# A decoder kernel on one core: the grouped attention stage with another order on TensorE, and moved preparation, rounding and end

## The chip, the cores and the metric

The kernel runs as one program on one core of a Trainium2 chip. The metric is device time in microseconds (us) of one execution. The median of three runs before the change is 1420.6 us (1420.59 to 1421.44). The engines are TensorE (PE in the profile, with its weight loads as PEld), VectorE (DVE), ScalarE (ACT), GpSimd (POOL) and SyncE (SP, which issues DMAs). They run their own instruction streams and meet only through semaphores.

## The reference, cut to what matters

Two decoder layers on 16 sequences of 128 tokens and 256 features, float32. Six steps follow each other, each adding to the residual x:

```python
x = x + L0_attn(layernorm(x))            # RWKV: token shift, three projections, a running maximum and two scans
x = x + L0_xattn(layernorm(x), ctx, ctx) # grouped attention: 32 query heads, 8 key heads, 8 features a head
x = x + L0_ffn(layernorm(x))             # dense part and 8 experts, top 2
x = x + L1_attn(layernorm(x))            # windowed attention with RoPE, 16 heads of 128
x = x + L1_xattn(layernorm(x), ctx)      # attention on a latent context
x = x + L1_ffn(layernorm(x))
```

The second step, which most of the change is about, is

```python
scores = einsum('bkgsd,bktd->bkgst', qh, kh) / sqrt(8)
out = einsum('bkgst,bktd->bkgsd', softmax(scores), vh)
```

## The kernel before, in words

Each step of the reference is one stage (a function and a block of five instruction streams): `rwkv`, `gqa`, `experts`, `windowed`, `cross` and the last feed forward. A stage begins on all engines when the one before has ended. The order of the work on each engine is written out by hand; a `wait_ge` on a semaphore count stands wherever an engine needs another's result.

**The stage `gqa`** runs over 16 blocks t of 128 tokens; each block has two halves of 16 heads, so 32 halves n. For each half: DVE normalises the block (`normalise`, L941, once a block), POOL splits it into a rounded and a rest part (`split_h`, L772 and L773), PE turns it (`turn_head`, L834), ACT takes it out of PSUM (`take_head`, L906), PE forms the scores in four pieces j of 512 columns in two PSUM banks in turn (`scores`, L843), DVE takes the extreme of each piece (`minimum`, L950). When both halves of a block are done, DVE splits the extremes in a rounded part (L958, a copy) and a rest (L960) (`split_least`), PE turns them (`turn_least`, L850) and ACT takes them out (`take_least`, L911). Then, three halves later than the scores (LEAD = 3), PE forms the scores again in turned form, less the extremes (`shifted_scores`, L859 and L863), ACT takes the exponents (`weigh`, L916, four per half), PE forms the weighed sums with a column of ones (`attend`, L871, into the one bank O), ACT takes them out (`take_out`, L922), PE turns them back into the same bank O (`turn_out`, L878), and DVE divides by the row sums (`divide`, a reciprocal L969 and a product L972). POOL adds the result to x.

PE's loop in step n is, in order: turned scores of n; scores pieces 0 and 1 of n+3; on odd n the turning of the extremes; weighed sums of n-1; scores piece 2; turning of a head part; scores piece 3; turning of the sums of n-1. `attend(n)` waits for the count `out_read` to reach n, that is for `divide(n-1)`, since bank O is shared. DVE's loop in step n begins with `divide(n-2)`, then the four minima of half n+3 (a normalisation behind the second on even n, a `bn_stats` behind the third on odd n), then on even n `split_least`. POOL's loop over t is: add of block t-2, split of block t+3, a copy of values, the key split of block t+4 and, in blocks 13 and 14, four products that fold norm weights into weights of the next stage (`fold_ffn0`).

The stage opens with the means and variances of all 16 blocks (L192), their scale on POOL, and the first normalisations.

**The stage `windowed`** runs over 16 blocks t with four key heads g. Here the change touches step g = 2 and 3: DVE's `rotate` (a sum L2366, a product with the cosines L2381, two with the sines L2383) and `take_weights` (a copy out of PSUM, L2404), which PE's `attend` (L2186) needs; POOL's `join` (L2062, for keys also L2065), `normalise` (L2072); ACT's `take_attended` (L2294) and `take_turned` (L2278), the latter needed by the scores of the next block (L2174, L2177).

Of the kernel before, what the change touches and what calls it, by code (L numbers as in the profile page):

```python
# [25 lines left out]
P = 128  # L26
# [188 lines left out]
def rwkv(nc, net, sem):  # L215
# [8 lines left out]
    with ExitStack() as ctx:  # L224
# [39 lines left out]
        own_dve, own_pool, own_act = sem("rw_own_dve"), sem("rw_own_pool"), sem("rw_own_act")  # L264
        block = ctx.enter_context(nc.Block("rwkv"))

        @block.sync
        def _(sp):
            load(nc, net)
            sp.wait_ge(net.keys_split, 1)  # L270
            sp.wait_ge(net.zeroed, 1)
            set_keys(sp, net, 0)
            sp.dma_start(net.later_keys[:].bitcast(F32), net.dram["ctx_keys"][:, 4:NB, :]).then_inc(net.keys_in[2], 16)
# [30 lines left out]
        def _(pool):  # L304
# [14 lines left out]
            split_keys(pool, Own(pool, net.own_keys), net, 0)  # L319
# [174 lines left out]
        def _(dve):  # L494
# [56 lines left out]
            def add(g):  # L551
                for i in range(2):
# [6 lines left out]
                    for j in (2 * i, 2 * i + 1):  # L559
                        dve.wait_ge(added, GB * g + j + 1)  # L560
                        dve.bn_stats(net.stats[:, GB * g + j, :], net.x[:, GB * g + j, :])
# [52 lines left out]
            def one(g, first, last):  # L614
# [11 lines left out]
                if not first and not last:  # L626
                    add(g - 1)
                own.again()
# [49 lines left out]
def gqa(nc, net, sem):  # L678
# [10 lines left out]
    VW, HALVES, LEAD = 32, 2 * NB, 3  # L689
    SLOTS, KEYS = 6, 4  # L690
# [4 lines left out]
    with ExitStack() as ctx:  # L695
# [23 lines left out]
        ones_set = sem("gq_ones_set")  # L719
# [18 lines left out]

        def set_by(t):

            return 64 * (t // 2) + 64

        @block.sync
        def _(sp):
            for t in range(1, NB):
                sp.wait_ge(keys_split, t + 1)
                if t >= 2:
                    sp.wait_ge(keys_set[t % 2], set_by(t - 2))
# [7 lines left out]
        def _(pool):  # L756
# [3 lines left out]
            def next_keys(t):  # L760

                if t >= KEYS:
                    pool.wait_ge(keys_set[t % 2], set_by(t - KEYS))
# [23 lines left out]
            scale_of(pool, own, net, scratch, aggregated, rstd_ready, 0, 1, WIDEN)  # L787
            split_h(0)
            scale_of(pool, own, net, scratch, aggregated, rstd_ready, 1, NB, WIDEN)
            pool.memset(least_parts[:].bitcast(F32), 0.0).then_inc(ones_set, 1)  # L790
            pool.wait_ge(net.keys_in[1], 16)
            next_keys(1)
            split_h(1)
            next_keys(2)
            split_h(2)
            pool.memset(values[:], 0.0).then_inc(ones_set, 1)
            pool.wait_ge(ones_set, 2)
            pool.memset(values[:, :, :, HD:HD + 1], 1.0).then_inc(ones_set, 1)
            pool.wait_ge(ones_set, 3)
            pool.wait_ge(net.in_ctx, 16)  # L800
            fetch_values(0)
            next_keys(3)
            for t in range(NB):
# [10 lines left out]
                if t in (NB - 3, NB - 2):  # L814
                    fold_ffn0(pool, net, t - NB + 3)
# [7 lines left out]
        def _(pe):  # L823
# [42 lines left out]
            def attend(n):  # L866
                pe.wait_ge(weighed, 4 * n + 4)
                pe.wait_ge(values_in, n // 2 + 1)
                need(pe, out_read, n)
                for v in range(4):  # L870
                    mm = pe.matmul(ps[32 * v:32 * v + VW, O, :], values[:, n // 2 % 2, 4 * (n % 2) + v, :],  # L871
# [3 lines left out]
            def turn_out(n):  # L875
                pe.wait_ge(out_taken, n + 1)
                for j in range(4):
                    mm = pe.transpose(ps[:, O, j * P:j * P + P], out_t[:, n % 2, j * P:j * P + P], ident)  # L878
                mm.then_inc(out_turned, 1)

            for n in range(-LEAD - 1, HALVES + 1):
                ahead = 0 <= n + LEAD < HALVES
                if 0 <= n < HALVES:
                    shifted_scores(n)
                if ahead:
# [4 lines left out]
                if n >= 1:  # L890
                    attend(n - 1)
# [6 lines left out]
                if n >= 1:  # L898
                    turn_out(n - 1)

        @block.scalar
        def _(act):
# [16 lines left out]
            def take_out(n):  # L919
                act.wait_ge(attended, n + 1)  # L920
                need(act, out_turned, n - 1)
                act.activation(out_t[:, n % 2], ps[:, O, :], ACT.Copy).then_inc(out_taken, 1)  # L922
# [15 lines left out]
        def _(dve):  # L938
# [14 lines left out]
            def split_least(t):  # L953
                parts = least_parts[:, t % 2].rearrange("p j (v c e) -> p c j v e", v=4, e=2)[:, 0:2]
                dve.wait_ge(topped, 8 * t + 8)
                dve.wait_ge(ones_set, 1)
                need(dve, least_turned, t - 1)
                dve.tensor_copy(parts[:, :, :, :, 0], least[:, t % 2]).then_inc(least_high, 1)  # L958
# [4 lines left out]
            def heads():  # L963
                return ps[:, O, :].rearrange("p (j g v) -> p g j v", j=4, v=VW)

            def divide(n):

                dve.wait_ge(out_turned, n + 1)
                dve.reciprocal(rsum[:, n % 2], heads()[:, :, :, HD]).then_inc(inverted, 1)  # L969
                dve.wait_ge(inverted, n + 1)  # L970
                need(dve, added, n // 2)
                dve.tensor_tensor(out[:, n % 2], heads()[:, :, :, 0:HD], wide(rsum[:, n % 2], [P, 4, 4, HD]),  # L972
                                  ALU.mult).then_inc(out_read, 1)

            def measure(t):
# [6 lines left out]
            dve.tensor_reduce(chosen[:], net.const[:, CONST["ident"]].rearrange("p (v c e) -> p c v e", v=4, e=2)[:, 0:2],  # L982
                              AX.XY, ALU.add).then_inc(tables_set, 1)
            dve.wait_ge(tables_set, 1)
            dve.tensor_scalar(minus[:], wide(chosen[:], [P, 2, P]), -1.0, None, ALU.mult).then_inc(tables_set, 1)
            dve.wait_ge(rstd_ready, 2)
            for t in (1, 2):
                normalise(t)
            for n in range(-LEAD, HALVES + 1):
                if n >= 2:  # L990
                    divide(n - 2)
                for j in range(4):
                    if n + LEAD < HALVES:
                        minimum(n + LEAD, j)
                    if j == 1 and n >= 0 and n % 2 == 0 and n // 2 + 3 < NB:
                        normalise(n // 2 + 3)
# [16 lines left out]
def fold_ffn0(pool, net, c):  # L1013

    if c == 0:
        pool.wait_ge(net.in_ffn0, 16 * 6)
    for tile, base, extra in ((net.gate0, PRE1, 1.0), (net.up0, PRE1, 1.0), (net.egu, PRE2, 1.0),
                              (net.router_w, RSCALE, float(D) ** -0.5)):
# [2162 lines left out]
```

## Time and profile before

| | |
|---|---|
| median of three runs | 1420.6 us |
| profiled execution | 1428.85 us |
| its span, first to last instruction | 1427.0 us |
| busy share of the span: PE, DVE, ACT, POOL | 86%, 68%, 53%, 42% |
| mean granted TensorE clock | 0.94 |
| stage `gqa` in the span | 136.8 to 309 us |
| stage `windowed`, its loop | about 600 to 1053 us |

Times of rows are microseconds from the span's start. In a row of the timeline the columns are start, length, engine, line, operation, result and operands, shape and count; in brackets stands how long the engine was idle before it and what ended that. A granted clock of 1.00 is 2.4 GHz, 0.50 is 1.2 GHz.

### The profile page before, as it was taken

What the parts mean: (1) busy time and instruction counts of PE and PEld (TensorE: products, weight loads), DVE (VectorE), ACT (ScalarE), POOL (GpSimd) and SP (SyncE); (2) the same over time, 40 slices, a digit from 0 to 9 for tenths busy, and PEclk for the clock granted to TensorE, in tenths of its full rate; (3) what the DMA queues carried; (4) which work ended last, traced back from release to release, by engine and by line L of the source; (5) the groups of instructions that cost most, each with busy time, mean ns of one, the idle gap of its engine ahead of it and who ended that gap; (6) DMA issues with size and microseconds to landing.
All of it is one profiled execution on the core that took longest, in us unless ns stands there. A gap on an engine that the chain in (4) does not pass through costs nothing. (4 is left out here: it accounts for less than half of the span.)

```text
span 1427.0 us, 24807 instructions
## 1 busy us (share of the span) xinstructions
PE 1228.8 (86%) x7726; PEld 944.8 (66%) x7726; DVE 965.2 (68%) x1864; ACT 760.5 (53%) x1755; POOL 605.0 (42%) x738
## 2 busy tenths in 40 slices
PE   6895899979988976389998999899987899969998
PEld 5673444448878865267776777777764565548887
DVE  5998799845755347877777777777764666643443
ACT  5432577753545455456666666666643555533332
POOL 2001555463055444576667666666653333320000
PEclk9997899968999997599999999999997999979999
DMA  9001000010025314200000000000000000000000
GB/s 326 1 0 48 19 16 16 9 60 1 5 85 156 100 51 167 107 0 1 2 0 0 0 0 0 0 0 0 1 1 4 5 3 3 3 1 1 15 15 31
DMA packets 27422, 44.74 MB, mean 31 GB/s; under 512 B 5648, under 2 KB 22160, under 8 KB 25936
## 3 DMA queue, kind: packets, MB, share of 16 engines
q1 hardware_dynamic: 23888, 34.31, 7.0%
q0 software_dynamic: 3456, 9.44, 2.5%
q8 instruction: 42, 0.69, 0.2%
q14 instruction: 36, 0.29, 0.1%
HBM read 32.21 MB, written 9.44 MB: 29 GB/s over the span
## 5 line engine op out<-in xcount | busy, mean ns | idle before, releaser
L2287 ACT ACTIVATE wi_weights<-wi_psum,wi_bias,wi_scale 128x128 f32<-128x128 f32 x256 | 113.9, 454 | 119.3 <-DVE wi_bias L2397 119.3
L2062 POOL TENSOR_TENSOR wi_straight<-wi_straight,wi_crossed 128x512 f32<-128x512 f32 x80 | 103.5, 1294 | 10.9 <-DVE wi_crossed L2383 10.8
L950 DVE TENSOR_REDUCE gq_least<-gq_psum 128x4 f32<-128x512 f32 x128 | 84.6, 686 | 15.9 <-PE gq_psum L843 14.2
L2050 POOL TENSOR_TENSOR wi_scratch<-wi_sums,wi_eps 128x4 f32<-128x4 f32 x80 | 35.3, 441 | 130.6 <-DVE wi_sums L2366 129.2
L2051 POOL TENSOR_TENSOR wi_scale<-wi_scratch,minus_half 128x4 f32<-128x4 f32 x80 | 84.6, 1058 | 6.3
L2388 DVE TENSOR_REDUCE wi_top<-wi_psum 128x4 f32<-128x512 f32 x64 | 44.0, 687 | 62.5 <-PE wi_psum L2177 62.5
L2186 PE MATMUL wi_psum<-wi_weights_t,wi_values 128*128 128x512 f32 x128 | 67.9, 612 | 20.5 <-DVE wi_weights_t L2404 20.5
L916 ACT ACTIVATE gq_weights_t<-gq_psum 128x512 f32<-128x512 f32 x128 | 67.6, 600 | 28.0 <-PE gq_psum L863 28.0
L2813 DVE TENSOR_REDUCE cr_top<-cr_psum 128x4 f32<-128x512 f32 x64 | 43.7, 682 | 46.2 <-PE cr_psum L2628 46.2
L2072 POOL TENSOR_TENSOR wi_weights<-wi_weights,wi_inverse 128x512 f32<-128x512 f32 x64 | 66.4, 1038 | 9.5 <-remote 5.1
L2177 PEld LDWEIGHTS wi_psum<-wi_k_t,wi_q_t 128*128 128x128 f32 x512 | 68.4, 194 | 1.7
L2177 PE MATMUL wi_psum<-wi_k_t,wi_q_t 128*128 128x128 f32 x512 | 68.0, 276 | 0.0
L2568 POOL TENSOR_TENSOR cr_keys_diagonal<-cr_qk,const 128x256 f32<-128x256 f32 x32 | 19.4, 627 | 112.1 <-ACT cr_qk L2740 112.1
L2128 PEld LDWEIGHTS wi_psum<-const,wi_straight 128*128 128x128 f32 x320 | 39.3, 142 | 41.5 <-issue 40.7
L1200 POOL DMA_INDIRECT ex_slot_rows<-ffn_rows,ex_token x40 | 38.8, 969 | 61.1 <-DVE ex_token L1699 39.4
L2383 DVE TENSOR_TENSOR wi_crossed<-wi_raw,wi_sin_q 128x256 f32<-128x256 f32 x128 | 62.7, 530 | 0.0
L843 PE MATMUL gq_psum<-gq_keys_diagonal,gq_h_t 128*128 128x512 f32 x128 | 58.3, 498 | 4.4 <-DVE gq_least L950 3.2
L3006 DVE TENSOR_TENSOR ff_gated<-ff_gated,ff_psum 128x512 f32<-128x512 f32 x32 | 22.0, 688 | 58.3 <-PE ff_psum L2926 57.9
L2381 DVE TENSOR_TENSOR wi_straight<-wi_raw,wi_cos_q 128x512 f32<-128x512 f32 x64 | 60.8, 950 | 0.0
L2259 ACT ACTIVATE wi_raw<-wi_psum 128x512 f32<-128x512 f32 x80 | 48.3, 603 | 20.3 <-PE wi_psum L2164 19.7
L2404 DVE COPY wi_weights_t<-wi_psum 128x512 f32<-128x512 f32 x64 | 43.7, 683 | 21.3 <-PE wi_psum L2142 21.3
L2351 DVE TENSOR_TENSOR wi_out_low<-wi_psum,wi_out_high 128x512 fp32r<-128x512 f32 x64 | 44.0, 688 | 18.6 <-ACT wi_out_high L2294 18.6
(413 smaller groups left out, 3797.1 us busy)
## 6 DMA issues: line engine op xcount, KB each, us to landing
slot_y<-ex_s_out SPq DMA_DIRECT2D x20, 256.0 KB
x<-in_x_dram SPq DMA_DIRECT2D x4, 512.0 KB, 7.6
gate<-in_gate_dram SPq DMA_DIRECT2D x2, 1024.0 KB, 6.1
up<-in_up_dram SPq DMA_DIRECT2D x2, 1024.0 KB, 8.1
down<-in_down_dram SPq DMA_DIRECT2D x2, 1024.0 KB, 10.4
egu<-in_egu_dram SPq DMA_DIRECT2D x1, 2048.0 KB, 14.7
gq_keys_diagonal<-gq_key_parts SPq DMA_DIRECT2D x64, 32.0 KB, 1.9
wo<-in_wo_dram SPq DMA_DIRECT2D x1, 2048.0 KB, 8.9
```

Source lines behind the costliest of these rows:

```text
L843: pe.matmul(ps[:, j % 2, :], h_t[:, n % SLOTS, j * P:j * P + P], kbd[n // 2 % KEYS][:, n % 2, :, :], start=True, stop=True).then_inc(score ...
L916: act.activation(weights_t[:, 4 * (n % 2) + v], ps[:, 2 + v, :], ACT.Exp, scale=-1.0).then_inc(weighed, 1)
L950: dve.tensor_reduce(least[:, n // 2 % 2, n % 2, j, :], ps[:, j % 2, :].rearrange("p (v t) -> p v t", t=P), AX.X, ALU.min).then_inc(topped, 1)
L2051: found = pool.tensor_tensor(scale[:, scale_at], scratch2[:], net.half[:, 0:4], ALU.pow)
L2062: added_up = pool.tensor_tensor(straight[:, at], straight[:, at], crossed[:, at], ALU.add)
L2072: pool.tensor_tensor(weights[:, g % 2], weights[:, g % 2], wide(inverse[:, g % 2], [P, 4, P]), ALU.mult).then_inc(normalised, 1)
L2177: mm = pe.matmul(bank[:, j * P:j * P + P], q_t[:, g % 2, j, :], k_t[:, s, g, :], start=False, stop=(j == 3), skip_group_check=True)
L2186: pe.matmul(ps[:, AV, :], values[:, s, g * DH:g * DH + DH], weights_t[:, g % 2], start=True, stop=True).then_inc(attended, 1)
L2259: act.activation(raw[:, at].rearrange("p j d -> p (j d)"), bank, ACT.Copy).then_inc(proj_taken, 1)
L2287: act.activation(weights[:, g % 2, j, :], ps[:, SC + g % 2, j * P:j * P + P], ACT.Exp, bias=bias[:, g % 2, j:j + 1], scale=scale[:, g, j:j ...
L2381: dve.tensor_tensor(straight[:, at], raw[:, at], over_heads(cos[:]), ALU.mult).then_inc(parts, 1)
L2383: dve.tensor_tensor(crossed[:, at, :, to], raw[:, at, :, source], over_heads(sin[:, to]), ALU.mult).then_inc(parts, 1)
```

## The change

In the first stage, DVE aggregates the statistics of the first four blocks as soon as they are there and POOL finds their scale; POOL also splits the keys of blocks 1 to 3 and SP sets the keys of block 1. In `gqa`, the opening therefore starts with three normalisations; two tables are made on ACT; the rounding L958 is a product with ones in place of a copy. On PE the weighed sums of n-1 move to stand right behind the turned scores of n, before all scores pieces. On ACT, `take_out` goes ahead of the last exponent and `take_least` behind it. The last halves use two further PSUM banks for the weighed sums and turn them back a step later. The folds are spread, one product a block, over blocks 4 to 11. In `windowed`, the two sine products of the next block's first query head move behind `take_weights(t, 2)`, and at g = 3 ACT takes the turned keys and queries before the weighed sums.

```diff
 # gqa
+        def out_bank(n):
+            return {HALVES - 3: 0, HALVES - 2: 1}.get(n, O)
...
             def attend(n):
                 pe.wait_ge(weighed, 4 * n + 4)
                 pe.wait_ge(values_in, n // 2 + 1)
-                need(pe, out_read, n)
+                if out_bank(n) == O:
+                    need(pe, out_read, min(n, HALVES - 3))
+                else:
+                    pe.wait_ge(topped, 4 * HALVES)
...
                 if 0 <= n < HALVES:
                     shifted_scores(n)
+                if n >= 1:
+                    attend(n - 1)
                 if ahead:
                     scores(n + LEAD, 0)
                     scores(n + LEAD, 1)
                 if n % 2 and 0 <= n + 1 < HALVES:
                     turn_least((n + 1) // 2)
-                if n >= 1:
-                    attend(n - 1)
...
-                if n >= 1:
+                if 1 <= n <= HALVES - 4:
                     turn_out(n - 1)
+                elif n >= HALVES - 2:
+                    turn_out(n - 2)
+            turn_out(HALVES - 1)
...
                     for v in range(3):
                         weigh(n, v)
+                if n >= 1:
+                    take_out(n - 1)
+                if 0 <= n < HALVES:
+                    weigh(n, 3)
                 if n % 2 and 0 <= n + 1 < HALVES:
                     take_least((n + 1) // 2)
-                if 0 <= n < HALVES:
-                    weigh(n, 3)
-                if n >= 1:
-                    take_out(n - 1)
...
-                dve.tensor_copy(parts[:, :, :, :, 0], least[:, t % 2]).then_inc(least_high, 1)
+                dve.tensor_tensor(parts[:, :, :, :, 0], least[:, t % 2],
+                                  net.ones[:, 0:KV_HEADS * 4].rearrange("p (c j v) -> p c j v", c=2, j=4),
+                                  ALU.mult).then_inc(least_high, 1)
...
-            aggregate(dve, net, aggregated)
-            dve.wait_ge(rstd_ready, 1)
-            normalise(0)
+            for t in range(3):
+                normalise(t)
...
-                if t in (NB - 3, NB - 2):
-                    fold_ffn0(pool, net, t - NB + 3)
+                if FOLD <= t < FOLD + 8:
+                    fold_ffn0(pool, net, t - FOLD)
 # rwkv
...
                     add(g - 1)
+                    if g == 1:
+                        measure_first()
...
+            for t in range(1, 4):
+                split_keys(pool, keys_own, net, t)
+            pool.wait_ge(normed, 1)
+            scale_of(pool, own, net, scratch, first_aggregated, first_rstd, 0, GB, float(HD))
 # windowed, ACT and DVE
...
                     weigh(t, g)
+                    if g == 3 and not last:
+                        take_turned("k", t + 1, 1 - s)
+                        take_turned("q", t + 1, 1 - s, 0)
                     if g > 0 or not first:
                         pt, _, pg = earlier(t, s, g, 1, U)
                         take_attended(pt, pg)
...
                     if g == 3:
                         take_weights(t, 2)
+                        if not last:
+                            rotate_crossed("q", t + 1, 1 - s, 0)
                     maximum(t, g)
```

## Rows read from the trace of the kernel before

**Rows 1.** Busy time by engine in the steady `gqa` loop; start:end, length, PE, PEld, DVE, ACT, POOL, PEclk, DMA, GB/s
```profile
166.00:275.00 109.00, 105.08 (x744) 54.07 (x740) 98.68 (x196) 86.27 (x162) 54.74 (x73) 1.00 0.07 16
```

**Rows 2.** Timeline of all engines, one pair of halves of the steady `gqa` loop
```profile
210.09 0.73 PE L843 MATMUL gq_psum<-gq_keys_diagonal,gq_h_t 128*128 128x512 f32 x2
...
210.63 1.29 DVE L950 TENSOR_REDUCE gq_least<-gq_psum 128x4 f32<-128x512 f32 x2
...
210.75 1.07 PE L871 MATMUL gq_psum<-gq_weights_t,gq_values 128*32 128x512 f32 x8
...
211.75 0.50 PE L843 MATMUL gq_psum<-gq_keys_diagonal,gq_h_t 128*128 128x512 f32 x1
...
211.84 0.41 DVE L941 TENSOR_SCALAR gq_h_tok<-x,mean_var,rstd 128x256 f32<-128x256 f32 x1
...
213.46 1.30 POOL L773 TENSOR_TENSOR gq_h_parts<-gq_h_tok,gq_h_parts 128x512 fp32r<-128x512 f32 x1
...
213.68 1.12 DVE L958 CAST gq_least_parts<-gq_least 128x32 fp32r<-128x32 f32 x1
...
215.25 0.29 DVE L972 TENSOR_TENSOR gq_out<-gq_psum,gq_rsum 128x128 f32<-128x128 f32 x1
...
217.23 0.69 DVE L950 TENSOR_REDUCE gq_least<-gq_psum 128x4 f32<-128x512 f32 x1 [0.49 <-PE gq_psum L843]
...
218.91 0.73 PE L843 MATMUL gq_psum<-gq_keys_diagonal,gq_h_t 128*128 128x512 f32 x2
...
219.05 0.29 DVE L972 TENSOR_TENSOR gq_out<-gq_psum,gq_rsum 128x128 f32<-128x128 f32 x1
```

**Rows 3.** Timeline, the stage's last half: the weighed sums behind the division
```profile
304.35 0.29 DVE L972 TENSOR_TENSOR gq_out<-gq_psum,gq_rsum 128x128 f32<-128x128 f32 x1
...
304.78 1.06 PE L871 MATMUL gq_psum<-gq_weights_t,gq_values 128*32 128x512 f32 x8 [0.77 <-DVE gq_out L972]
```

**Rows 4.** Instructions of line L958: shortest, median and longest, in ns
```profile
L958 DVE CAST gq_least_parts<-gq_least x16: 199/1120/1318, 153.1 to 287.0; 128x32 fp32r<-128x32 f32 x16
```

**Rows 5.** Timeline of POOL and DVE in `windowed`, one step g = 2
```profile
948.68 1.27 POOL L2062 TENSOR_TENSOR wi_straight<-wi_straight,wi_crossed 128x512 f32<-128x512 f32 x1
948.83 1.67 DVE L2381 TENSOR_TENSOR wi_straight<-wi_raw,wi_cos_q 128x512 f32<-128x512 f32 x1
...
950.03 1.37 POOL L2065 TENSOR_TENSOR wi_straight<-wi_straight,wi_scale 128x512 f32<-128x512 f32 x1
...
950.42 1.60 DVE L2383 TENSOR_TENSOR wi_crossed<-wi_raw,wi_sin_q 128x256 f32<-128x256 f32 x2
```

**Rows 6.** Timeline of PE near the end of `gqa`: two stalls, and a slow instruction
```profile
278.13 0.66 PE L850 MATMUL gq_psum<-const,gq_least_parts 128*128 128x128 f32 x4 [1.64 <-DVE gq_least_parts L960]
...
289.85 1.11 PE L850 MATMUL gq_psum<-const,gq_least_parts 128*128 128x128 f32 x4 [2.29 <-DVE gq_least_parts L960]
...
290.89 1.94 PE L871 MATMUL gq_psum<-gq_weights_t,gq_values 128*32 128x512 f32 x8
```

**Rows 7.** Busy time and granted clock right behind the first of those stalls
```profile
279.00:282.40 3.40, 3.40 (x15) 1.69 (x8) 1.78 (x4) 1.87 (x4) 0.38 (x1) 0.50 0.00 0
```

**Rows 8.** Timeline, the opening of `gqa` on DVE
```profile
136.82 1.17 DVE L192 BATCH_NORM_AGGREGATE mean_var<-stats 128x2 f32<-128x6 f32 x16 [0.31 <-PEq L224]
...
144.06 1.62 DVE L941 TENSOR_SCALAR gq_h_tok<-x,mean_var,rstd 128x256 f32<-128x256 f32 x2 [4.41 <-POOL rstd L198]
```

**Rows 9.** Timeline of PE and POOL in `windowed`, from step g = 3 into the next block
```profile
952.09 1.26 POOL L2062 TENSOR_TENSOR wi_straight<-wi_straight,wi_crossed 128x512 f32<-128x512 f32 x1 [0.70 <-DVE wi_crossed L2383]
...
952.67 1.12 PE L2186 MATMUL wi_psum<-wi_weights_t,wi_values 128*128 128x512 f32 x2 [1.32 <-DVE wi_weights_t L2404]
...
956.21 1.04 POOL L2072 TENSOR_TENSOR wi_weights<-wi_weights,wi_inverse 128x512 f32<-128x512 f32 x1
957.03 0.39 PE L2174 MATMUL wi_psum<-wi_mask,wi_ident 128*128 128x512 bf16 x1 [0.98 <-ACT wi_q_t L2278]
...
958.14 0.60 PE L2142 MATMUL wi_psum<-const,wi_weights 128*128 128x128 f32 x4
```

More of the change, by code:

```diff
@@ L269, in _ @@
             load(nc, net)
-            sp.wait_ge(net.keys_split, 1)
+            sp.wait_ge(net.keys_split, 4)
             sp.wait_ge(net.zeroed, 1)
-            set_keys(sp, net, 0)
+            for t in range(2):
+                set_keys(sp, net, t)
             sp.dma_start(net.later_keys[:].bitcast(F32), net.dram["ctx_keys"][:, 4:NB, :]).then_inc(net.keys_in[2], 16)
@@ L560, in add, with measure_first @@
                         dve.wait_ge(added, GB * g + j + 1)
-                        dve.bn_stats(net.stats[:, GB * g + j, :], net.x[:, GB * g + j, :])
+                        own.did(dve.bn_stats(net.stats[:, GB * g + j, :], net.x[:, GB * g + j, :]))
+            def measure_first():
+                own.wait()
+                dve.wait_ge(shift_ready, 1)
+                for b in range(GB):
+                    dve.bn_aggr(net.mean_var[:, b, :], net.stats[:, b, :]).then_inc(first_aggregated, 1)
             def statistics(g):
@@ L689, in gqa @@
     VW, HALVES, LEAD = 32, 2 * NB, 3
+    FOLD = 4
     SLOTS, KEYS = 6, 4
@@ L744, in _ @@
         def _(sp):
-            for t in range(1, NB):
+            for t in range(2, NB):
                 sp.wait_ge(keys_split, t + 1)
-                if t >= 2:
-                    sp.wait_ge(keys_set[t % 2], set_by(t - 2))
+                sp.wait_ge(keys_set[t % 2], set_by(t - 2))
                 if t >= KEYS:
@@ L977, in measure @@
                 dve.bn_stats(net.stats[:, t, :], net.x[:, t, :])
-            aggregate(dve, net, aggregated)
-            dve.wait_ge(rstd_ready, 1)
-            normalise(0)
+            for t in range(3):
+                normalise(t)
             dve.tensor_reduce(chosen[:], net.const[:, CONST["ident"]].rearrange("p (v c e) -> p c v e", v=4, e=2)[:, 0:2],
[L983 to L988, printed above, removed]
+                              AX.XY, ALU.add).then_inc(chosen_set, 1)
+            for b in range(GB, NB):
+                dve.bn_aggr(net.mean_var[:, b, :], net.stats[:, b, :]).then_inc(aggregated, 1)
             for n in range(-LEAD, HALVES + 1):
@@ L995, in _ @@
                     if j == 1 and n >= 0 and n % 2 == 0 and n // 2 + 3 < NB:
+                        if n == 2:
+                            dve.wait_ge(rstd_ready, 1)
                         normalise(n // 2 + 3)
@@ L2306, in one @@
                         take_turned("q", t, s, g + 1)
-                    elif not last:
-                        take_turned("k", t + 1, 1 - s)
-                        take_turned("q", t + 1, 1 - s, 0)
                     if g == 0 and not last:
@@ L2374, in rotate @@
                     dve.wait_ge(turned, number("q", t - 1, g + 2) + 1)
-                cos, sin = (tables[f"{n}_{what}"] for n in ("cos", "sin"))
-                half = DH // 2
+                cos = tables[f"cos_{what}"]
                 def over_heads(table):
@@ L2381, in rotate, with rotate_crossed, over_heads @@
                 dve.tensor_tensor(straight[:, at], raw[:, at], over_heads(cos[:]), ALU.mult).then_inc(parts, 1)
+            def rotate_crossed(what, t, s, g):
+                if what == "v":
+                    return
+                n, at = of_five(what, t, g), slot(what, g)
+                sin, half = tables[f"sin_{what}"], DH // 2
+                def over_heads(table):
+                    return table.unsqueeze(1).broadcast_to([P, 4, table.shape[-1]])
                 for to, source in ((slice(0, half), slice(half, DH)), (slice(half, DH), slice(0, half))):
```

62 lines of the change are left out of this document (32 added, 30 removed).

## The prediction

> **What bounds the kernel now.** I read the page first: PE is busy for most of the span, so its order matters more than anyone else's load. Then the busy time by stretch for the steady loop of `gqa`: PE works 105.08 of 109 us [rows 1], so 3.92 us are idle; at 8.82 us a pair of halves (from one pair of scores to the same pair two halves on, 210.09 to 218.91) [rows 2] that is 0.32 idle and 8.50 worked in a pair. The loop of today is bound by PE, with DVE close behind at 98.68. Last the timeline of one pair, to see what lies between a result and its use: the reader is to see that the weighed sums (210.75) run while DVE takes the first two minima (210.63 for 1.29). PE's long instruction covers DVE's work and the other way round.
>
> **What the new order does.** Both loops are written out, so the chain follows from the code. The weighed sums of n-1 wait for `divide(n-2)`, because bank O is shared; DVE does that division at the head of its step n, behind the last minimum of its step n-1 and, every second half, behind the split of the extremes. Before, two scores pieces, and every second time a turning, ran ahead of the weighed sums while DVE finished. Now nothing but the turned scores does, and all scores of n+3 are queued behind the waiting weighed sums on PE. So DVE waits for scores, scores wait for the weighed sums, these wait for DVE's division: one ring through both engines. That such a wait is real and how fast it is answered is seen once in the last half: the product ends at 304.64 and the sums, idle 0.77 for it, start at 304.78, 0.14 later [rows 3].
>
> **The ring, priced.** From one start of the weighed sums to the next, with a normalisation and a split in between: sums to the scores behind them 1.00 (210.75 to 211.75); scores to first minimum 0.54 (210.09 to 210.63); two minima 1.21 (210.63 to 211.84); from the normalisation to the end of the division 3.70 (211.84 to 215.25 and 0.29) [rows 2]; answer 0.14 [rows 3]. Sum 6.59. The other half: 1.00, 0.54, 1.21, then from the third minimum to the end of the division 2.11 (217.23 to 219.05 and 0.29) [rows 2], 0.14: sum 5.00. A pair takes 11.59 in place of 8.82, 2.77 more. PE has 8.50 to do in it and idles 3.09: per half (8.50 less the 0.66 of a turning [rows 6]) / 2 = 3.92 of work; behind the first scores piece it waits some 0.62 for a minimum (0.54, 0.64 and 0.1 less the 0.66 of two pieces), so it is ready at 4.54 of 6.59 and idles 2.05 in one piece, and 0.42 in the other half, where the turning fills the gap. Of the 15 pairs 13 have the full pattern: 13 x 2.77 = **+36.0**.
>
> **The new rounding.** The copy L958 takes 0.20 alone and 1.12 at the median [rows 4]. It starts 0.22 into POOL's L773 (213.46 for 1.30) and ends 0.04 behind it [rows 2]. The change puts a product of two tensors in SBUF in its place. In the other attention stage such a product (L2381, 948.83 for 1.67) starts 0.15 into a POOL product and ends 0.55 behind that one's end at 949.95 [rows 5]: it is held as the copy is. So I give the new rounding nothing. If it escaped, 1.12 - 0.20 = 0.92 a pair came back. The split still meets L773: minima 3 and 4 follow the normalisation on DVE as they do now, and POOL is started by the same normalisation. The Trainium skill speaks against the edit too (SBUF — State Buffer, section Who interferes with whom): a DVE instruction with two SBUF inputs contends with a GpSimd instruction that reads SBUF, and the one that comes second blocks. By this rule the loop is the 11.59 above, and the rows agree; without it, it would be 10.67.
>
> **The clock.** Behind PE's stall of 1.64 the granted clock was 0.50 for 3.4 us [rows 6, 7], and behind the stall of 2.29 a set of weighed sums took 1.94 in place of 1.07 [rows 2, 6]. The new idle piece of 2.05 lies between these two, in each pair. A fall just then sits on the ring: 0.87 on the sums and some on the scores. I take 1.2 each in three pairs of four, 13 x 0.75 x 1.2 = **+11** rounded down; ends 0 (the clock holds) and +26 (each pair, with most of its PE work at the low level).
>
> **The beginning.** The 1.17 of statistics and DVE's 4.41 of waiting for the scales [rows 8] go, 5.6 at most. But the first scores still wait for POOL's split of block 0 and its turning, and `normalise(2)` now waits for that split; DVE's first minimum comes about 2.5 earlier, and step 1, whose sums have no division ahead, about 1 better: **-3.5**, between 0 and -5.6. In the first stage DVE aggregates four blocks, 4/16 of 1.17 = 0.3 [rows 8], and POOL's three key splits may hold a DVE product once, a POOL instruction's 1.3 [rows 5]: **+0.4**, up to 1.7. SP's four more transfers are issued ahead of keys not needed before block 4, and the tables moved to ACT meet an idle ACT; if not, some tenths.
>
> **The end and the folds.** The stalls of 1.64 and 2.29 [rows 6] come from the split held by the folds of blocks 13 and 14. Spread, a fold stands behind a key split on POOL, where it holds back an add that has a pair's time. 3.9 come back, and the two further banks spare about 1 more, the last steps being then bound by ACT's four exponents: **-5**, between 0 and -9. Taking the extremes behind the last exponent costs nothing: PE needs them at the next turned scores, over 1 us later; uncovered it would be an exponent's 0.6 a pair.
>
> **The windowed stage.** With the sine products behind it, the copy `take_weights` starts when L2381 ends, 950.50, and PE's wait of 1.32 [rows 9] goes. The products lose nothing: they are held by POOL's L2065 until 951.40 anyway [rows 5], and the copy, which reads PSUM, fits in that time. So POOL's join (952.09) and all of its chain stay where they are, up to `normalise`, which ends at 957.25 [rows 9]. On ACT, queries taken first remove the 0.98 ahead of the next block's scores. What is late next is that POOL result: the turning of the weights, now at 958.14, can start at about 957.4 [rows 9]. That is 0.73 a block, not 2.3; x 15 = **-11**. Ends: 0.35 (the copy does push the join back) and 0.98, 5 to 15.
>
> **Sum** against the profiled execution of 1428.85: 36.0 + 11 - 3.5 + 0.4 - 5 - 11 = +27.9, 1456.8. The runs lie 8.2 below that execution, so 1420.6 + 27.9 = **1448.5**.
>
> **Rivals.**
> - The clock holds: 11 less, 1437.5. For it: the idle pieces are separate and PE is busy in between; against it: it fell behind 1.64.
> - The clock falls in each pair and for longer: 15 more, 1463.
> - The split escapes POOL: a pair is 10.67, 13 x 1.85 = 24.1, PE's longest idle piece is 1.1, and the clock holds: 24.1 - 3.5 + 0.4 - 5 - 11 = +5.0, 1425.6. Against it: the held product of rows 5.
> - **Faster:** the division is done when PE asks. Then PE's order alone counts, 8.50 and the 0.62 behind the first scores piece, 9.12 a pair: 13 x 0.30 = +3.9, and 3.9 - 3.5 + 0.4 - 5 - 11 = -15.2, 1405.4. It decides at the point where the division ends within the time of the turned scores, some 0.7 behind the turning of the sums; DVE's last minimum and the split stand in front of it, so I see no way but that DVE gets its scores much earlier than the code says.
> - The order on PE makes no difference on balance (a gain in one stage equal to the loss in the other): near 1420.
>
> **How the numbers follow.** Forecast 0.59, clock holds 0.13, clock longer 0.10, split escapes 0.08, faster 0.07, no difference 0.03. The likeliest gives 1448.5, by itself 1441 to 1457 from the ends of its small terms. Leaving out the two last cases and half of the longer clock, the range is 1425 to 1465. A measurement of this kernel can tell about 0.2%, 2.8 us, from no change: faster 0.07, same 0.03, slower 0.90.
>
> **What would show it.** In the profile after: weighed sums (L871's group) idle for DVE's product in nearly every half, some 2.0 and 0.4 in turn, and starts in pairs 11.6 or more apart; DVE idle some 1.7 a half for scores; the new rounding as long as the copy; granted clock under 1 within the loop; no stalls by folds at the end; in `windowed` blocks 0.7 shorter, with the turning of the weights waiting for POOL. It is wrong if the weighed sums don't wait, or if pairs stay near 9.

## The result and the profile after

The changed kernel takes 1453.5 us (1452.68 to 1456.15), the kernel before 1420.8 us (1420.59 to 1421.44) in the same comparison: 1.0233 times as long, 95% interval 1.0215 to 1.025. The forecast was 1448.5. The profiled execution of the changed kernel took 1452.68 us, with a span of 1450.8. One of the six executions of wi_norm (below) took 1604.6 us at a mean granted clock of 0.72, a slow state, and is left out of its median.

Groups of instructions of after by line, from the list of all groups (count, then busy time, mean ns of one, and the idle time of the engine in front of them with what ended it): the minima, the scores, the weighed sums.

```profile
L975 DVE TENSOR_REDUCE gq_least<-gq_psum 128x4 f32<-128x512 f32 x128 | 84.0, 687 | 62.3 <-PE gq_psum L858 61.8
...
L858 PE MATMUL gq_psum<-gq_keys_diagonal,gq_h_t 128*128 128x512 f32 x128 | 64.1, 545 | 11.0 <-DVE gq_least L975 8.9 <-ACT gq_h_t L927 1.6
...
L889 PE MATMUL gq_psum<-gq_weights_t,gq_values 128*32 128x512 f32 x256 | 37.4, 654 | 30.4 <-DVE gq_out L999 28.0 <-ACT gq_weights_t L937 2.4
```

The same three groups of the kernel before, from the same view:

```profile
L950 DVE TENSOR_REDUCE gq_least<-gq_psum 128x4 f32<-128x512 f32 x128 | 84.6, 686 | 15.9 <-PE gq_psum L843 14.2
...
L843 PE MATMUL gq_psum<-gq_keys_diagonal,gq_h_t 128*128 128x512 f32 x128 | 58.3, 498 | 4.4 <-DVE gq_least L950 3.2 <-ACT gq_h_t L906 1.2
...
L871 PE MATMUL gq_psum<-gq_weights_t,gq_values 128*32 128x512 f32 x256 | 37.3, 658 | 0.8 <-DVE gq_out L972 0.8
```

The three arcs of the ring are there: sums wait for DVE's division (28.0 us in place of 0.8), the minima for scores (61.8 in place of 14.2), scores for minima (8.9 in place of 3.2). One pair of halves in the timeline of after, which answers to [rows 2]:

```profile
231.58 1.28 POOL L793 TENSOR_TENSOR gq_h_parts<-gq_h_tok,gq_h_parts 128x512 fp32r<-128x512 f32 x1
231.59 1.33 DVE L983 TENSOR_TENSOR gq_least_parts<-gq_least,ones 128x32 fp32r<-128x32 f32 x1
...
233.37 0.29 DVE L999 TENSOR_TENSOR gq_out<-gq_psum,gq_rsum 128x128 f32<-128x128 f32 x1
...
233.81 1.42 PE L889 MATMUL gq_psum<-gq_weights_t,gq_values 128*32 128x512 f32 x8 [2.02 <-DVE gq_out L999]
...
235.16 1.22 PE L858 MATMUL gq_psum<-gq_keys_diagonal,gq_h_t 128*128 128x512 f32 x2
...
235.99 1.29 DVE L975 TENSOR_REDUCE gq_least<-gq_psum 128x4 f32<-128x512 f32 x2 [2.33 <-PE gq_psum L858]
...
237.97 0.63 PE L849 MATMUL gq_psum<-const,gq_h_parts 128*128 128x128 f32 x4 [0.31 <-issue]
...
239.76 0.29 DVE L999 TENSOR_TENSOR gq_out<-gq_psum,gq_rsum 128x128 f32<-128x128 f32 x1
...
240.20 1.06 PE L889 MATMUL gq_psum<-gq_weights_t,gq_values 128*32 128x512 f32 x8 [0.26 <-DVE gq_out L999]
...
241.73 1.29 DVE L975 TENSOR_REDUCE gq_least<-gq_psum 128x4 f32<-128x512 f32 x2 [1.68 <-PE gq_psum L858]
```

Read it from the rounding L983: it starts 0.01 behind POOL's product and ends 0.06 behind its end. The division follows, PE has idled 2.02 for it, and right after that idle piece the weighed sums take 1.42 and two pieces of scores 1.22, where the next half's sums take 1.06 and those of before 1.07 and 0.73 [rows 2].

The starts of the weighed sums in the timelines give the length of each half. Sums n are the weighed sums of half n, and the half with the split is the one in which DVE also splits the extremes; 13 pairs lie between sums 1 and sums 27. The split half of the last pair differs and is left out of the first column (6.26 in before, behind a stall of [rows 6], and 5.32 in after), as are the last pair's other halves of before (5.47) and pe_act_back (4.01). The runs named here follow below:

| kernel | half with the split | other half | from sums 1 to sums 27, us |
|---|---|---|---|
| before | 4.94 | 3.87 | 117.5 |
| after | 6.60 | 5.12 four times, 6.34 to 6.70 nine times | 163.3 |
| before_pe_new | 6.58 | 5.25 three times, 6.28 to 6.86 ten times | 166.8 |
| pe_back | 4.95 | 5.37 | 133.5 |
| pe_act_back | 4.95 | 3.88 | 114.3 |
| fill | 6.61 | 5.12 | 151.6 |
| norm_late | 5.65, once 7.52 | 5.12 to 5.14 seven times, 5.74 to 5.77 four times, 6.6 twice | 147.0 |

### The profile page after: what moved, and what is told of

The parts are those of the page before. It is cut to its first block and busy times, and to the rows that moved or that the text cites. A ratio compares the mean times of both kernels' runs of the same rounds, so it can differ in the third digit from the quotient of the medians.

```text
span 1450.8 us, 24766 instructions
## 1 busy us (share of the span) xinstructions
PE 1226.3 (85%) x7679; PEld 948.0 (65%) x7726; DVE 962.4 (66%) x1863; ACT 761.5 (52%) x1757; POOL 602.9 (42%) x737
## 5 line engine op out<-in xcount | busy, mean ns | idle before, releaser
L975 DVE TENSOR_REDUCE gq_least<-gq_psum 128x4 f32<-128x512 f32 x128 | 84.0, 687 | 62.3 <-PE gq_psum L858 61.8
L792 POOL TENSOR_TENSOR gq_h_parts<-gq_h_tok,ones 128x512 fp32r<-128x512 f32 x16 | 17.0, 1062 | 152.4 <-PE gq_psum L849 92.3
L858 PE MATMUL gq_psum<-gq_keys_diagonal,gq_h_t 128*128 128x512 f32 x128 | 64.1, 545 | 11.0 <-DVE gq_least L975 8.9
L2153 PE MATMUL wi_psum<-const,wi_straight 128*128 128x128 f32 x320 | 49.8, 279 | 18.3 <-POOL wi_straight L2087 10.9
L889 PE MATMUL gq_psum<-gq_weights_t,gq_values 128*32 128x512 f32 x256 | 37.4, 654 | 30.4 <-DVE gq_out L999 28.0
```

The source lines that it names most:

```text
L858: pe.matmul(ps[:, j % 2, :], h_t[:, n % SLOTS, j * P:j * P + P], kbd[n // 2 % KEYS][:, n % 2, :, :], start=True, stop=True).then_inc(score ...
L975: dve.tensor_reduce(least[:, n // 2 % 2, n % 2, j, :], ps[:, j % 2, :].rearrange("p (v t) -> p v t", t=P), AX.X, ALU.min).then_inc(topped, 1)
L2153: mm = pe.transpose(ps[:, bank_of(what, g), j * P:j * P + P], straight[:, slot(what, g), j, :], ident)
```

## The experiments

Times are medians; each is compared with runs of the kernel before on the same chip, 1420.7 to 1421.8 us.

**The kernel before, once more (before_again).**

> The kernel before, profiled once more. In its first profile the stage of the experts took 277.3 us (309.4 to 586.7), in the profile of the changed kernel 266.4 us, though the change touches nothing in it; and that first profiled execution (1428.85) lies 8 us above the other runs. If the stage was only disturbed in that one execution, it takes about 266 here and the span is near 1419. If the spread folds (moved out of the end of the stage before it) make the stage of the experts shorter, it takes about 277 again and the span is near 1427.

Measured: 1421.73 us, span 1419.9, and the stage of the experts took 268.7 (its first product at 309.18, the next stage's at 577.89). The first profiled execution was long in that one stage, so it was right of the prediction to take 8.2 us off. In the profiles of the changed kernel and of all the kernels below it takes 266 to 273, with no edit in it; a single profile can't settle differences of a few us there. The second profile is the better partner for after, part by part (the first stage ends with its last statistics on DVE, the opening with sums 1, the experts and `windowed` begin with their first product):

| part | forecast | second profile of before to after |
|---|---|---|
| first stage | +0.4 | +0.3 (136.38 to 136.70) |
| opening of `gqa`, to sums 1 | -3.5 | -3.7 (30.15 to 26.41) |
| ring, clock, folds and end | +42 | +41.7 (163.26 - 117.44 = +45.8 up to sums 27, then -4.1) |
| experts | 0 | -2.3 |
| `windowed` | -11 | -4.9 |
| the two last stages | 0 | -0.2 |
| sum | +27.9 | +30.9 |

**TensorE's order alone put back (pe_back), and alone put in (before_pe_new).**

```diff
 # pe_back: after
-                if n >= 1:
-                    attend(n - 1)
                 if ahead:
                     scores(n + LEAD, 0)
                     scores(n + LEAD, 1)
                 if n % 2 and 0 <= n + 1 < HALVES:
                     turn_least((n + 1) // 2)
+                if n >= 1:
+                    attend(n - 1)
 # before_pe_new: the opposite, in the kernel before
```

> The kernel before with TensorE's weighed sums alone moved to stand right behind the turned scores. Theory: this edit alone makes the ring, so pairs go from 8.8 to about 11.7, the clock falls as in the changed kernel, and the time rises by 40 to 50 us, to 1461 to 1471 (more than the changed kernel's, since beginning and end stay the old ones). Rival, the ring needs ScalarE's new order or the new rounding as well: less than 20 us more, below 1441.

Measured: 1470.4 us, 1.0353 (1.0335 to 1.0371), 49 us more: the edit alone makes a loss as large as that of the two orders together (48 us, by pe_act_back below), with the old rounding and ScalarE's old order.

> The changed kernel, with TensorE's weighed sums put back behind the turning of the extremes; all else of the change stays. Theory (a ring through VectorE: sums wait for the division, scores for the sums, minima for the scores): the pairs go back from 11.7 to about 8.9 and the granted clock stays at 1.00, so the time falls by 40 to 46 us, to 1407 to 1414; up to 0.4 in every second half may stay, 5 us in all, because ScalarE still takes the extremes last. Rival, the new rounding or ScalarE's order makes the loop slow: the time stays above 1440. Rival, the sums' place costs only the clock: 1440.

Measured: 1428.6 us, 1.0059 (1.0042 to 1.0076). 25 us come back, not 40 to 46, and a pair takes 10.32, not 8.9. The timeline of pe_back shows why, in the half without the split:

```profile
220.48 0.66 PE L865 MATMUL gq_psum<-const,gq_least_parts 128*128 128x128 f32 x4 [0.44 <-DVE gq_least_parts L987]
...
221.06 1.06 PE L889 MATMUL gq_psum<-gq_weights_t,gq_values 128*32 128x512 f32 x8
...
222.19 0.60 ACT L943 ACTIVATE gq_out_t<-gq_psum 128x512 f32<-128x512 f32 x1 [1.21 <-PE gq_psum L889]
...
222.69 0.59 ACT L937 ACTIVATE gq_weights_t<-gq_psum 128x512 f32<-128x512 f32 x1
...
223.16 0.61 ACT L932 ACTIVATE gq_least_t<-gq_psum 128x512 fp32r<-128x512 f32 x1
...
223.87 0.63 PE L849 MATMUL gq_psum<-const,gq_h_parts 128*128 128x128 f32 x4 [1.32 <-issue]
```

The extremes and the parts of h are turned into the same bank (TR). With ScalarE's new order the extremes are taken out behind the last exponent, that behind the taking of the sums, and that behind the sums themselves; the turning of the next part starts 0.10 after the extremes are out (223.77), and PE has idled 1.32. The profile calls this wait "issue", since it shows nothing that ended it. So ScalarE's order costs 10.32 - 8.82 = 1.5 a pair where the sums come late. In the changed kernel, where they come first, the wait is 0.31 (237.97 above), and before_pe_new, with ScalarE's old order, has it too: PE idles 14.2 us in all ahead of the head turnings in after and 14.9 there, both put down to "issue". So no run shows a cost of ScalarE's order in the changed kernel.

**Both orders put back (pe_act_back).** As pe_back, and in ScalarE's loop

```diff
-                if n >= 1:
-                    take_out(n - 1)
-                if 0 <= n < HALVES:
-                    weigh(n, 3)
                 if n % 2 and 0 <= n + 1 < HALVES:
                     take_least((n + 1) // 2)
+                if 0 <= n < HALVES:
+                    weigh(n, 3)
+                if n >= 1:
+                    take_out(n - 1)
```

> The changed kernel with both orders of the steady loop undone: TensorE's weighed sums behind the turning of the extremes, and on ScalarE the extremes taken ahead of the last exponent and the sums' take_out behind it. With TensorE's order alone undone a pair took 10.3 (steps of 5.36 and 4.96 in turn), since the turning of a head part waited for the bank that the extremes are taken from, behind the last exponent. Theory, the two orders are all that makes the loop slower: pairs go back to 8.8, and with the gains of the beginning, the end and the spread folds the time is 1403 to 1410, below the kernel before. Rival, the new rounding or the spread folds cost something in the loop too: pairs of 9.2 and more, 1413 and above.

Measured: 1405.8 us, 0.9884 (0.9863 to 0.9906). Pairs are 8.83 again. The group of head turnings shows the wait come and go, in pe_back:

```profile
L849 PE MATMUL gq_psum<-const,gq_h_parts 128*128 128x128 f32 x128 | 20.6, 285 | 24.9 <-issue 18.7 <-POOL gq_h_parts L793 6.3
```

and in pe_act_back:

```profile
L849 PE MATMUL gq_psum<-const,gq_h_parts 128*128 128x128 f32 x128 | 20.6, 287 | 6.7 <-POOL gq_h_parts L793 6.4 <-issue 0.3
```

All that the change does besides the two orders (opening, rounding, folds, end, windowed stage) gains 15 us; the two orders cost 48.

**The idle piece filled (fill).** On odd n from 3 to 27, between turned scores and weighed sums:

```diff
+    FILL = 4
...
+            def fill(n):
+                pe.wait_ge(h_taken, n + LEAD + 1)
+                for _ in range(FILL):
+                    pe.matmul(ps[:, TR, :], h_t[:, (n + 1) % SLOTS, 0:P], kbd[(n + 1) // 2 % KEYS][:, 0, :, :],
+                              start=True, stop=True)
```

> The changed kernel, with four products of 512 columns, whose result nobody uses, added on TensorE between the turned scores and the weighed sums of every second half (odd n from 3 to 27), in the place where TensorE idles for 2.0 us. They start with what is there and take some 1.4 at most, so they don't stand on the ring. Theory, the lower clock behind the idle piece costs 1.2 to 1.6 us in 9 of 13 pairs: with the piece filled the clock holds at 1.00, the short halves all take 5.1, and the time falls by 9 to 14 us, to 1440 to 1444. Rival, the clock's fall lies beside the waits and costs nothing: the time stays at 1453 (or rises, if the added products push the sums back).

Measured: 1445.6 us, 1.0183 (1.0163 to 1.0203), 8 us less than after. In the windows (start:end, length, PE, PEld, DVE, ACT, POOL, PEclk, DMA, GB/s) the changed kernel has, behind an idle piece and over the same steady stretch as [rows 1],

```profile
235.00:238.00 3.00, 2.69 (x12) 1.76 (x9) 1.59 (x3) 1.69 (x3) 1.26 (x2) 0.53 0.20 44
...
166.00:275.00 109.00, 81.61 (x511) 43.64 (x509) 70.49 (x136) 59.30 (x110) 49.33 (x60) 0.89 0.05 12
```

and the filled one

```profile
228.00:231.40 3.40, 3.14 (x20) 1.67 (x20) 1.84 (x3) 1.67 (x3) 2.46 (x3) 1.00 0.12 27
166.00:275.00 109.00, 90.55 (x597) 48.10 (x597) 76.99 (x149) 65.16 (x121) 52.70 (x65) 1.00 0.05 12
```

whose timeline has

```profile
228.03 1.07 PE L890 MATMUL gq_psum<-gq_weights_t,gq_values 128*32 128x512 f32 x8 [0.91 <-DVE gq_out L1008]
```

With the idle piece cut from 2.02 to 0.91 the clock stays at 2.4 GHz, every short half takes 5.12, and sums 27 come 11.7 us earlier after sums 1. Useless work bought time. The total moved by less, since experts and `windowed` took 2.8 and 2.0 longer in the profiled execution than in that of after, with no edit in them.

**The rounding: a copy again (copy_back), and out of POOL's way (norm_late).**

```diff
 # copy_back
-                dve.tensor_tensor(parts[:, :, :, :, 0], least[:, t % 2],
-                                  net.ones[:, 0:KV_HEADS * 4].rearrange("p (c j v) -> p c j v", c=2, j=4),
-                                  ALU.mult).then_inc(least_high, 1)
+                dve.tensor_copy(parts[:, :, :, :, 0], least[:, t % 2]).then_inc(least_high, 1)
 # norm_late
-                    if j == 1 and n >= 0 and n % 2 == 0 and n // 2 + 3 < NB:
-                        if n == 2:
-                            dve.wait_ge(rstd_ready, 1)
-                        normalise(n // 2 + 3)
...
                     split_least((n + LEAD) // 2)
+                if n >= 0 and n % 2 == 0 and n // 2 + 3 < NB:
+                    if n == 2:
+                        dve.wait_ge(rstd_ready, 1)
+                    normalise(n // 2 + 3)
```

> The changed kernel with the rounding of the extremes made by a copy again, in place of the product with ones. Theory, both are held by GpSimd's product for as long as it runs: no difference, 1451 to 1456. Rival, the product with two operands in SBUF is held where a copy would not be, or less: 1430 to 1445. Rival, the copy is held longer: above 1458.

Measured: 1456.8 us, 1.0248 (1.0229 to 1.0266), whose interval overlaps that of after: no difference shown. Its loop is no longer than that of after (161.4 from sums 1 to sums 27).

> The changed kernel, with VectorE's normalisation of a block moved behind the split of the extremes, so that GpSimd's products on that block start after the split and not beside it. Theory, the new rounding is held by GpSimd's product (1.33 in place of some 0.2) and stands on the ring: without it the half with the split takes about 5.5 in place of 6.6; TensorE's idle piece shrinks from 2.0 to about 1, so the clock holds more often: 14 us from the ring and up to 11 from the clock, 1428 to 1440. Rival, the rounding is as long by itself, being a product of two tensors: no change, 1453. Rival, the split is faster but the ring then waits for the scores or the exponents: 1445 and above.

Measured: 1439.6 us, 1.0132 (1.0114 to 1.015). The rounding's shortest, median and longest ns, in after, copy_back and norm_late:

```profile
L983 DVE TENSOR_TENSOR gq_least_parts<-gq_least,ones x16: 215/1332/1347, 150.6 to 330.5; 128x32 fp32r<-128x32 f32 x16
```

```profile
L983 DVE CAST gq_least_parts<-gq_least x16: 199/1317/1323, 151.1 to 332.8; 128x32 fp32r<-128x32 f32 x16
```

```profile
L983 DVE TENSOR_TENSOR gq_least_parts<-gq_least,ones x16: 213/220/220, 150.3 to 313.4; 128x32 fp32r<-128x32 f32 x16
```

Product and copy are held alike, and neither is slow by itself. Unheld, the half with the split takes 5.65, 0.95 less, 11 us over twelve pairs; with what the clock gives back the loop is 16.2 shorter. The rest of the hoped gain went into a wait that the edit made, seen in norm_late:

```profile
226.40 1.12 POOL L1045 TENSOR_SCALAR up<-up,fvec 128x1024 f32<-128x1024 f32 x1
...
227.49 0.73 POOL L804 TENSOR_TENSOR x<-x,gq_out 128x256 f32<-128x256 f32 x1
...
228.32 0.29 DVE L999 TENSOR_TENSOR gq_out<-gq_psum,gq_rsum 128x128 f32<-128x128 f32 x1 [0.68 <-POOL x L804]
228.76 1.07 PE L889 MATMUL gq_psum<-gq_weights_t,gq_values 128*32 128x512 f32 x8 [0.89 <-DVE gq_out L999]
```

POOL starts its split later, so the fold and the add behind it on POOL are late, and the division must wait for its buffer. It takes the fold as well: the wait stands in the six halves behind the folds of 1.12 (5.74 to 5.77 in the table) and of 1.97 (6.6), and in none behind the two folds of 0.28 or without a fold.

**The same edit on the old order (both_back_norm)** makes that wait decide.

> The changed kernel with both orders of the steady loop undone and the normalisation moved behind the split of the extremes. Theory, with the old order TensorE bounds the loop (8.50 of work in 8.82), so a split that is 1.1 shorter on VectorE gives back at most the 0.32 of idle time in a pair: 0 to 4 us less than without it, 1401 to 1406. Rival, the split's length counts in the old order as well: more than 8 us less, 1397 or below.

Measured: 1417.5 us, 0.9971 (0.9955 to 0.9986), 12 us worse than without it; both guesses missed. Its timeline, in a block with a fold:

```profile
196.69 1.12 POOL L1045 TENSOR_SCALAR gate<-gate,fvec 128x1024 f32<-128x1024 f32 x1
197.79 0.72 POOL L804 TENSOR_TENSOR x<-x,gq_out 128x256 f32<-128x256 f32 x1
198.61 0.29 DVE L999 TENSOR_TENSOR gq_out<-gq_psum,gq_rsum 128x128 f32<-128x128 f32 x1 [2.02 <-POOL x L804]
...
199.05 1.93 PE L889 MATMUL gq_psum<-gq_weights_t,gq_values 128*32 128x512 f32 x8 [1.74 <-DVE gq_out L999]
```

Fold, add, division, sums: the fold that is free in the changed kernel is on the path here, and the idle 1.74 is again followed by sums at the low clock; of the six idle pieces of 1.68 to 2.57 in this loop three are followed by a fall of the clock. Before the first fold its pairs took 9.0, close to the 8.83 without the edit.

**The windowed stage alone (before_wi).** The kernel before with the two windowed edits of the change.

> The kernel before with the two edits of the windowed stage alone. The prediction gave them 0.73 a block, 11 us: 1410. The traces of before and after show blocks shorter by less than 0.1, since VectorE's small product for the bias (0.15 by itself) now runs into GpSimd's join and takes 0.73, so the exponents start no earlier, and the sums taken last delay VectorE's next split. By that the stage gains 0 to 4 us: 1416 to 1421.

Measured: 1418.0 us, 0.9976 (0.9965 to 0.9987): 2 to 5 us gained. Blocks, from one block's first score to the next one's, go from 28.81 to 28.75 in the steady loop, 0.9 us over 13 blocks; another 2.4 come at the stage's end (58.9 in before and 56.5 here, from the first maximum of the last block but one to the stage's last instruction). No run has the two edits apart. PE's wait for the turned weights did go, as the groups of before and after show:

```profile
L2186 PE MATMUL wi_psum<-wi_weights_t,wi_values 128*128 128x512 f32 x128 | 67.9, 612 | 20.5 <-DVE wi_weights_t L2404 20.5
```

```profile
L2211 PE MATMUL wi_psum<-wi_weights_t,wi_values 128*128 128x512 f32 x128 | 68.1, 613 | 2.8 <-DVE wi_weights_t L2439 1.3
```

What came instead stands in the timeline of after, the stretch of [rows 9] (POOL's join at 952.09 there is 978.49 here, so the two time scales differ by 26.40):

```profile
978.49 1.26 POOL L2087 TENSOR_TENSOR wi_straight<-wi_straight,wi_crossed 128x512 f32<-128x512 f32 x1 [0.70 <-DVE wi_crossed L2418]
...
979.05 0.73 DVE L2432 SCALAR_TENSOR_TENSOR wi_bias<-wi_top,wi_scale 128x4 f32<-128x4 f32 x1
...
983.17 0.69 DVE L2376 TENSOR_TENSOR wi_out_low<-wi_psum,wi_out_high 128x512 fp32r<-128x512 f32 x1 [1.28 <-ACT wi_out_high L2319]
...
984.01 0.60 PE L2167 MATMUL wi_psum<-const,wi_weights 128*128 128x128 f32 x4
984.07 0.84 DVE L2363 TENSOR_SCALAR wi_h_tok<-x,mean_var,rstd 128x256 f32 x1 [0.21 <-issue]
...
984.83 0.68 DVE L2423 TENSOR_REDUCE wi_top<-wi_psum 128x4 f32<-128x512 f32 x1
```

and the same instructions of before:

```profile
953.25 0.16 DVE L2397 SCALAR_TENSOR_TENSOR wi_bias<-wi_top,wi_scale 128x4 f32<-128x4 f32 x1
...
955.84 0.69 DVE L2351 TENSOR_TENSOR wi_out_low<-wi_psum,wi_out_high 128x512 fp32r<-128x512 f32 x1 [0.31 <-ACT wi_out_high L2294]
...
956.74 0.66 DVE L2338 TENSOR_SCALAR wi_h_tok<-x,mean_var,rstd 128x256 f32 x1 [0.21 <-issue]
...
958.34 0.69 DVE L2388 TENSOR_REDUCE wi_top<-wi_psum 128x4 f32<-128x512 f32 x1 [0.95 <-PE wi_psum L2177]
```

The turning of the weights starts 26.40 - (984.01 - 958.14) = 0.53 earlier, of the 0.73 that were forecast. It stands on PE behind the next block's scores, and these still wait for the queries: PE idles 30.3 us for them in before and 32.8 in before_wi. But ScalarE takes the sums last, DVE's split of them starts 0.93 later, the normalisation behind it too, and the next block's first maximum, queued behind both, starts 0.09 later than before, no longer waiting for scores. Two runs test this.

**The normalisation out of that queue (wi_norm)**, before_wi with

```diff
-                    if g == 0 and not last:
-                        normalise(t + 1, 1 - s)
...
                     shift(t, g)
+                    if g == 0 and not last:
+                        normalise(t + 1, 1 - s)
```

> The kernel before with the two edits of the windowed stage, and with VectorE's normalisation of the next block moved from the head of step g = 0 to behind that step's bias product. Theory, the half microsecond that the new order gains at the turning of the weights is lost because the sums, taken last, delay VectorE's split of them by 0.9, and the normalisation and the next block's first maximum are queued behind it: with the normalisation out of the way the maximum starts some 0.5 earlier, blocks go from 28.75 to 28.2 to 28.4 and the time from 1418 to 1410 to 1414. Rival, GpSimd's chain of the block sets its length: blocks stay at 28.75 and the time at 1418. Rival, the next block's head part is late through the later normalisation: slower than 1421.

Measured: 1410.2 us, 0.9931 (0.9903 to 0.9958); blocks 28.29. The maximum of wi_norm waits for scores again, though the bias product is held as in after:

```profile
966.48 0.73 DVE L2407 SCALAR_TENSOR_TENSOR wi_bias<-wi_top,wi_scale 128x4 f32<-128x4 f32 x1
...
971.64 0.69 DVE L2398 TENSOR_REDUCE wi_top<-wi_psum 128x4 f32<-128x512 f32 x1 [0.35 <-PE wi_psum L2177]
```

So the queue on DVE was what ate most of the gain.

**The bias product freed (wi_late)**, before_wi with the sine products behind `shift(t, 3)`.

> The kernel before with the two edits of the windowed stage, but with the two sine products one place further back, behind the maximum and the bias product. The bias product then meets no product of GpSimd and takes 0.15, and the exponents start some 1.4 earlier; GpSimd's join starts some 0.9 later. Theory, GpSimd is busy from the join to the end of the block without a gap, so its later start is what is late: blocks longer by 0.3 to 0.9, 5 to 13 us more than with the edits as they are, 1423 to 1431. Rival, the exponents set the block's length (the held bias product is then what ate the gain): blocks shorter by 0.4 or more, 1412 or less.

Measured: 1422.3 us, 1.0001 (0.9986 to 1.0015); blocks 28.85, between the two expectations. The bias product took 0.16 and counted from the copy `take_weights` and against wi_norm, the exponents started 1.5 earlier and the join 0.55 later (not 0.9); blocks became 0.10 longer than in before_wi. The held product is therefore not the limit of the block; that POOL's chain alone is, isn't shown either.

**Together (best):** pe_act_back and wi_norm.

> The changed kernel with both orders of the steady loop undone, and with the windowed stage's normalisation behind the bias product of step g = 0. The first gave 1405.8, the second blocks shorter by 0.47 over 15 blocks. Theory, the two stages follow each other and their gains add: 1396 to 1401. Rival, part of the windowed gain was a difference between executions: 1402 to 1406.

Measured: 1398.3 us, 0.9846 (0.9824 to 0.9867), faster than both kernels.

## Why the prediction was right, and where it was not

- **The ring**: right. Priced 6.59 and 5.00, measured 6.60 and 5.12; in the half of 5.12 the way from the first minimum to the end of the division takes 3.44 (229.56 to 233.00 in fill) for the 1.21 and 2.11 of the price. The 6.59 held though the rounding took 1.33 in place of the row's 1.12: it ends when POOL's product does, 2.96 behind the start of the normalisation that sets POOL off, in before (211.84 to 214.80) as in after (229.96 to 232.92). Twelve full pairs and a last one of 10.45 give 12 x (11.72 - 8.82) + 1.63 = 36.4 before the clock, for 36.0; that the two are so close is luck, a pair being 0.13 dearer and the full pairs 12 and not 13. Idle pieces were 2.02 and 0.26, for 2.05 and 0.42. before_pe_new and pe_act_back show that the order on PE makes it.
- **The rounding at nothing**: right, and for the reason given (copy_back, norm_late). By the Trainium skill (SBUF — State Buffer, section Who interferes with whom) a DVE instruction with two SBUF inputs contends with a GpSimd instruction that reads SBUF. The trace agrees, with 1.33 for the product beside POOL's product and 0.22 for it alone.
- **The clock**: right. 1.2 in three pairs of four was estimated; it was 1.2 to 1.6 in nine of 13, together 12.2 for 11, and fill took 11.7 of it away. That the clock falls was read from rows; the share of pairs was a guess, and that it came out is luck.
- **Opening, folds, end**: within their bounds, though no run has them alone. The stalls of [rows 6] are gone, and folds and end give 2.8 + 4.1 = 6.9 for 5 (2.8 is what before's 117.4 has over 13 pairs of 8.82). The opening's 3.7 is uncertain: the profiles with the new opening reach sums 1 24.6 to 30.1 us behind the first stage, those with the old one 29.5 to 31.3, while the low clock lasts 6.8 to 23.9 us in the new ones.
- **ScalarE's order**: the price of nothing held in this kernel, the reason was wrong. The prediction said that PE needs the extremes only at the next turned scores. PE needs their bank sooner, for the turning of the next part, which costs 1.5 a pair in pe_back, not an exponent's 0.6; the sums' new place hides it here.
- **The windowed stage**: wrong, 2 to 5 us by before_wi where 11 were forecast. The step that failed is "what is late next is that POOL result". The 0.98 that PE waits for the queries was counted as removed, but that wait stayed (30.3 us in all before, 32.8 in before_wi), and the turning of the weights is queued behind it. Who waits for the sums, now taken last on ScalarE, was not asked. DVE's split does, and the next maximum is queued behind it. With that queue mended (wi_norm) the blocks lose 0.52, most of the 0.73. That the bias product would be held by the join that it now meets was missed too; freeing it (wi_late) made no block shorter, but moved the join as well, so its price stays open.
- The forecast, 1448.5, lies 5 below the result; the windowed term alone is 6 to 9 too good, and the small misses of the other terms partly make up for it.

## What to carry to other kernels

Before an instruction that waits is moved ahead in a queue, follow what is queued behind it until you come back to what it waits for: a ring's length is the sum of its arcs over both engines, whatever each engine's busy share, and rows of the old trace price it well. Of each instruction moved back, ask who waits for its result and for the buffer that it frees; a wait removed from the most loaded engine (20.5 us here) gains only where the next instruction in every queue is free to follow.

## What the runs showed of the hardware that was not expected

- Filling an idle piece of TensorE with products nobody uses made the kernel 8 us faster: of twelve idle pieces of 2.02 to 2.04 nine were followed by a stretch at 1.2 GHz (granted clock 0.50), of the twelve pieces of 0.90 to 0.94 in fill none.
- A small VectorE product of four columns took 0.73 in place of 0.15 while a GpSimd product of 512 columns ran, and a copy of 32 columns with one tensor in SBUF was held just as the product with two (1.32 and 1.33 in place of 0.20 and 0.22).
